# A window-attention network and a binary convolution on one core: the places of all stages in each engine's order laid out anew

## The reference

```python
x0 = layernorm(x + attn(x, x, x))                 # self, full image
x1 = layernorm(a + attn(a, a, a))  # a = avgpool4(x0): the low image
q  = layernorm(x0 + attn(x0, patches(x1), patches(x1)))   # cross
o  = layernorm(q + relu(q @ w1 + b1) @ w2 + b2)
y  = conv3x3(sign(clip(o)), sign(weight))         # 9 taps
out = o + batchnorm(y)                            # over all 8 images
```

## Time and profile before

| | |
|---|---|
| time, median of 3 runs | 2183.79 us (2181.91 to 2187.62) |
| the profiled execution's own time | 2176.89 us |
| its span from first to last instruction | 2175.1 us |
| PE busy | 1997.8 us, 92% |
| PE busy while self units stand alone and start up (first 200 us) | 168.15 us |
| PE busy from 858 to 1030 us, between two images' ends | 172.00 of 172.00 us |
| busy: DVE, ACT, POOL | 73%, 63%, 57% |
| last pass, hardly any PE work (2100 us to the end) | 75 us |

### The profile page before, as it was taken

One profiled execution on the slowest core, in us unless ns is written; L12 is line 12 of the kernel. 1 busy time (PEld: TensorE's weight loads), 2 busy tenths in 40 slices (PEclk: granted clock), 3 DMA queues, 4 the chain that ended last, 5 costly groups with the idle time before them and its releaser, 6 DMA issues.

```text
span 2175.1 us, 93188 instructions
## 1 busy us (share of the span) xinstructions
PE 1997.8 (92%) x39504; PEld 1604.3 (74%) x39504; DVE 1577.2 (73%) x5093; ACT 1364.9 (63%) x2531; POOL 1247.3 (57%) x1280
## 2 busy tenths in 40 slices
PE   6998889999899999999999998999999999999950
PEld 4886777887788877888778886888778877677730
DVE  3997867777677777787777777777767776666545
ACT  3765656666566665666666665666656666566545
POOL 4665656666566655665566665666556665555410
PEclk9999999999999999999999999999999999999985
DMA  6877755665566655666556656666656664555539
GB/s 178 231 220 199 218 157 166 193 188 151 169 184 181 188 171 164 180 182 185 156 175 197 178 151 179 181 179 192 172 163 179 176 192 129 145 148 148 181 102 410
DMA packets 335053, 393.56 MB, mean 181 GB/s; under 512 B 39984, under 2 KB 239408, under 8 KB 334640
## 3 DMA queue, kind: packets, MB, share of 16 engines
q1 hardware_dynamic: 333792, 386.61, 60.0%
q10 hardware_dynamic: 848, 0.99, 0.1%
HBM read 208.29 MB, written 160.27 MB: 169 GB/s over the span
## 4 chain that ended last, share of the span: by engine, by line
PE 81%; DVE 7%; ACT 4%; DMA 3%; issue 3%; POOL 2%; SPq 0%; POOLq 0%; DVEq 0%; ACTq 0%
PE ps_hid L702 11%; PE ps_y L714 10%; PE ps_o L650 9%; PE ps_proj L565 9%; PE ps_s L631 7%; PE ps_hid L733 6%; PE ps_y L682 5%; PE ps_s L637 5%; PE ps_max L621 5%; PE ps_y L669 4%; PE ps_proj L590 3%; PE ps_t L690 2%; PE ps_t L663 2%; PE ps_t L722 1%; DVE negmax L927 1%
## 5 line engine op out<-in xcount | busy, mean ns | idle before, releaser
L1086 POOL TENSOR_TENSOR prob_lo<-prob,prob_hi 128x512 f16<-128x512 f32 x528 | 611.5, 1158 | 641.1 <-ACT prob_hi L800 640.9
L927 DVE TENSOR_REDUCE negmax<-ps_max 128x8 bf16<-128x512 f32 x528 | 359.4, 681 | 195.1 <-PE ps_max L621 190.2
L799 ACT ACTIVATE prob<-ps_s 128x512 f32<-128x512 f32 x528 | 314.3, 595 | 204.7 <-PE ps_s L637 195.3
L939 DVE TENSOR_TENSOR onorm<-ps_o,rden 64x128 f32<-64x128 f32 x1056 | 304.8, 289 | 25.5
L800 ACT ACTIVATE prob_hi<-ps_s 128x512 f16<-128x512 f32 x528 | 312.6, 592 | 0.0
L838 ACT ACTIVATE hid<-ps_hid,columns_sb 128x512 f32<-128x512 f32 x256 | 176.0, 688 | 209.5 <-PE ps_y L714 116.5
L650 PE MATMUL ps_o<-vb,prob_hi 128*128 128x68 f16 x4224 | 288.9, 195 | 7.5 <-POOL prob_lo L1086 3.8
L631 PEld LDWEIGHTS ps_s<-qs,ks 64*64 64x64 f16 x8448 | 174.1, 109 | 147.1 <-issue 117.9
L702 PE MATMUL ps_hid<-xf,w_sb 128*128 128x512 f32 x512 | 275.5, 620 | 3.3 <-ACT yconv L857 2.2
L650 PEld LDWEIGHTS ps_o<-vb,prob_hi 128*128 128x128 f16 x4224 | 229.1, 98 | 43.0 <-issue 18.8
L714 PE MATMUL ps_y<-w_sb,hid 128*128 128x128 f32 x2048 | 252.5, 275 | 0.0
(11 more groups left out here) (112 smaller groups left out, 3419.4 us busy)
## 6 DMA issues: line engine op xcount, KB each, us to landing
k_rows<-k_flat SPq DMA_DIRECT2D x256, 256.0 KB, 3.2
qs<-q_rows SPq DMA_DIRECT2D x512, 128.0 KB, 3.2
ks<-k_rows SPq DMA_DIRECT2D x128, 512.0 KB, 4.4
q_rows<-q_flat SPq DMA_DIRECT2D x128, 256.0 KB, 2.4
vb<-v_flat SPq DMA_DIRECT2D x128, 136.0 KB, 3.3
vb<-values_out SPq DMA_DIRECT2D x128, 136.0 KB, 3.3
xin<-in_x SPq DMA_DIRECT2D x64, 256.0 KB, 4.5
self_out<-xa SPq DMA_DIRECT2D x64, 256.0 KB, 3.1
```

What stands on the lines that cost most here:

```text
L799: activation(prob[:, pair_no(u, k) % 2, :], ps_s[:, :], ACT.Exp)
L927: v.tensor_reduce(negmax[:, pair_no(u, k) % 2, :], ps_max[:, :].rearrange("p (a t) -> p a t", t=TOK), AX.X, ALU.max, negate=True).then_inc ...
L939: done = v.tensor_tensor(onorm[r, u.seq % 2, k, :].rearrange("p (w j d) -> p j w d", w=2, j=4), blocks[r, :, :, DH * h2:DH * h2 + DH], r2[ ...
L1086: g.tensor_tensor(prob_lo[:, i, :], prob[:, i, :], prob_hi[:, i, :], ALU.subtract).then_inc(s_prob, 1)
```

## The change

Nearly all entries of five tables (`SELF`, `CROSS`, `LOW`, `LAST_CONV`, `PAIR`) get new values, and one constant changes; no operation, transfer, buffer, wait condition or loop is touched. `LOW_AFTER` goes from 17 to 20, but units come in steps of 4 and 8 places there, and all 136 units, the low ones among them, keep their place.

```diff
-LOW_AFTER = 17
+LOW_AFTER = 20
-CROSS = dict(load=-10.84, q_put=-8.03, k_put=-7.53, q=-7.49, k_take=-6.97, q_hi=-6.85, q_move=-6.39, q_lo=-6.21,
-             v_fetch=-5.99, k_move=-5.72, bias=-4.22, turn=4.36, turned=4.68, resid=5.52, stats=5.59, project=5.64,
...
+CROSS = dict(load=-10.31, q_hi=-7.29, q=-7.23, q_lo=-7.02, k_take=-6.46, q_put=-6.32, q_move=-5.03, k_put=-4.49,
+             k_move=-3.1, v_fetch=-1.87, bias=-0.63, turned=4.4, turn=4.71, resid=5.18, stats=5.84, project=5.97,
...
-LAST_CONV = dict(conv_take=15.25, conv=15.82, conv_stats=16.56)
-
-PAIR = dict(rough=-2.02, exp=-1.22, scores=-1.03, prob_lo=-0.81, weigh=0.02)
+LAST_CONV = dict(conv_take=14.95, conv=15.04, conv_stats=26.71)
+
+PAIR = dict(rough=-1.99, exp=-1.19, scores=-0.99, prob_lo=-0.18, weigh=0.19)
```

26 lines of the change are left out of this document (13 added, 13 removed).

## The result

| | before | after |
|---|---|---|
| median of the runs, us | 2185.5 (2181.9 to 2187.6, 4 runs) | 2150.5 (2147.1 to 2152.3, 4 runs) |
| profiled execution, us (span) | 2176.9 (2175.1) | 2149.8 (2148.0) |
| ratio, 95% interval | | 0.984 (0.982 to 0.986) |

The kernel became faster, by 35 us in the medians and by 27 us between the two profiled executions. The forecast was 2157 us with a range of 2143 to 2176, and 27 us for the profiled execution.

The account below looks back on a forecast made before the run. TensorE was taken to bound the kernel (92% busy, no gaps between images), with idle time at images' ends. Terms -18.4 - 5 + 3.5 - 11 - 4 - 4 + 2 + 9 + 1 = -27 gave 2157 us, range 2143 to 2176.

Parts of the forecast that it names:

- Key wait: Before low units' rough scores: TensorE's wait for keys goes, -18.4 us, and its lost clock, -5; +3.5 comes back.
- +3.5: After a low unit, the next cross unit's keys (c18's) come 0 to 1 us late at each of 7 images.
- Image projections: Low unit's key and value projections through one PSUM bank: -1.4 us per image, +0.7 at kk0 included; -11 in all.
- The low unit's spread: At an image's end, c17's out no longer waits for the bank spread used: -0.5 us at 8 images, -4.
- rival (a): All waits at images' ends go, neither c18's keys nor k behind kk0 late: sum about -40, 2144 us; chance 0.16.
- Self-only stretch: First 150 us, self units alone: the wait before project shrinks, -0.35 us for 11 units, -4; bounds -9 and 0.
- first cross units: Where cross units start: c0's key put stands behind its query fetch and v_fetch comes later, +2 us; bounds 0 and +5.
- Switches: Regular stretches between images: more changes between 16-bit and fp32 stages on TensorE, 0.16 us each, +9; bounds +5 and +12.
- h3 to f3: Regular stretches: f3 needs h3's relu after 1.82 us and has 1.86; +1 us for jitter, bounds 0 and +10.
- (c): Rival: transfers bind at more places (first cross units, c18, self-only stretch), +9 us on the sum, 2166; chance 0.17.
- (d): Rival: f3 waits for h3's relu behind spread's copy (0.77 us) in every regular stretch, up to 2200 us; chance 0.07.
- (b): Rival: the key wait changes hands, the low unit's queries arriving as late: sum about -4, 2180 us; chance 0.08.

Follow-up runs that it names:

- e10: Kernel before with only the two halves of a cross unit's queries moved earlier on ACT and DVE: 2167.2 us, ratio 0.9908.
- e2: Kernel after with only the low unit's key fetch put back behind its query fetch and the next cross unit's query put: 2151.2 us.
- e1: Kernel before with only the low unit's key fetch moved right behind its own key put on SP: 2172.9 us, ratio 0.9937.

## Why the prediction held, and where its steps did not

1. **Key wait, -18.4 - 5 + 3.5 = -16.9.** The size was low and the mechanism half right. The key wait went from every low unit and the clock came back there (1.00 in the window), as said. What failed first is the sentence that put the cause in the fetch's place ("the fetch stood behind c18's put") and took the earlier half on DVE only as a guard against a new wait: e10 and e2 show that it was the cause. What failed next is what comes back. The +3.5 for c18's late keys never came, since c18's put is early by itself; in e1, where it isn't, that wait is there (1.08 us). In its place came the weigh's wait for POOL, 1.28 us at an end, which no term had. From c17 to c18 the gain of 3.28 us is 2.09 of the keys' wait, 1.70 of clock (an estimate: 4.1% of 41.37 us), 0.68 of smaller waits that no term had either, less 1.28. In the mean of five ends 2.95 us were gained, 3.2 without the dearer stretch, against 23.4 / 8 - 3.5 / 7 = 2.4. And the 9 waits were not those of eight low units and one other, but of l1 to l7, c1 and c26.
2. **Image projections, -1.4 per image.** Measured -1.74 out of an end, -2.0 without the dearer stretch. The bank's 2.54 us and the 0.4 of the weigh were right to 0.03 us. The +0.7 at kk0 came too, as 0.60 us before k of s35, but in the step ahead, across the end; without it the term is -2.1.
3. **The low unit's spread, -0.5.** Measured -0.72, or -1.0 without the dearer stretch, with kk0's wait inside. Out's wait of 0.69 us went, and spread now waits 0.50 for its own normalising. Terms 1 to 3 together: an end gained 5.41 + 3 x 0.28 = 6.25 us, against 2.4 + 1.4 + 0.5 = 4.3. Over 8 ends that is some 15 us more, and as much as rival (a) had (49.4 / 8 = 6.2).
4. **Self-only stretch, -4, first cross units +2.** Both wrong. The wait before project went, and the unit stayed at 11.6 us. The first cross units cost +4.9, at the bound of 5: the head of SP's queue waited for the low values' store, whose place went from 9.4 to 15.53 and which the prediction never priced. "v_fetch comes later" was costed as a late arrival; it was a stop for the queue behind it. A part of the 4.9 is clock: 0.88 in that step, some 3.4 us as an estimate (12% of 27.6), where before had 1.00.
5. **Switches, +9, and h3 to f3, +1.** The exchanges of neighbours cost 0.13 us for 0.16. h3 to f3 was the step that failed: I had 1.86 us against a need of 1.82, and it was 1.80, so that f2 and f3 together wait 0.15 us in every stretch. The mistake is in h3's 0.93 + 0.03: behind spread it stands behind an fp32 stage, which by term 5's own price takes 0.075 off, and it was 0.861. That is some 8 us, near that term's upper bound of 10. With them a stretch costs 0.28 more in the median and 0.36 in the mean.
6. **From the profiled execution to the median.** I added the 6.9 us by which before's profiled execution lay under its median, as if they belonged to both kernels. After's lies 0.7 under. That took 6 us from the forecast, and the clock says what they may be. Before's profiled execution had a mean granted clock of 0.979; in the 34 executions of before that were timed beside the experiments it was 0.969 to 0.976, the median 0.973, and in after's four 0.978 to 0.980. So the kernel before usually loses more to the lower clock than its trace shows, and after does not: up to (0.979 - 0.973) x 2185 = 13 us as an estimate, beside the 8 by which the medians gained more than the traces. The -5 for clock was read from a lucky execution. No second trace of before shows where the rest falls, so this cause is argued and not shown.

So 15 us more at the ends were paid back by 4 (self-only), 3 (first cross units) and 7 (f2 and f3): a right sum of terms that erred both ways. Of the rivals, (a) held at the ends, (c) at the first cross units, (d) at 0.15 of its 0.77 us; (b) occurred at l0 alone, whose first rough score waits 1.1 us for its queries. The right time is luck in part: errors of 15 and 14 us that cancel. The direction and the order of size are not.
